# Attention's weighted sum in a decoder layer: one float32 product per head in 32-column tiles, in place of block-diagonal products of split values

## The reference, cut to what matters

```
x = x + attn(layernorm(x))                       # stage A
qh, kh, vh = split(x' @ Wq + bq), split(ctx @ Wk + bk), split(ctx @ Wv + bv)   # 16 heads of 32
scores = einsum('bhqd,bhkd->bhqk', qh, kh) / sqrt(32), causal mask
attn   = softmax(scores)                         # over 77 keys
out    = einsum('bhqk,bhkd->bhqd', attn, vh)     # the weighted sum of the values
x = x + merge(out) @ Wo + bo                     # stage B
x = x + mixture_of_experts(layernorm(x))         # stage C
```

## Time and profile before

| | |
|---|---|
| median of 3 runs | 1202.05 us (1202.03 to 1203.4) |
| span of the profiled execution | 1203.6 us |
| PE busy | 1143.6 us (95%), 5889 products |
| DVE busy | 937.9 us (78%) |
| ACT busy | 737.5 us (61%) |
| POOL busy | 459.2 us (38%) |
| chain that ended last | PE 72%, DVE 9%, DMA 6%, issue 5% |

### The profile page before, as it was taken

How to read it: one execution, slowest core, us unless ns; L and a number is a source line. 1 busy time by engine, 2 the same in 40 slices (tenths; PEclk the granted TensorE clock), 3 DMA queues, 4 the chain that set the end, 5 groups by cost and what they waited for, 6 DMA issues and landing times.

```text
span 1203.6 us, 24087 instructions
## 1 busy us (share of the span) xinstructions
PE 1143.6 (95%) x5889; PEld 962.8 (80%) x5890; DVE 937.9 (78%) x2195; ACT 737.5 (61%) x2114; POOL 459.2 (38%) x412
## 2 busy tenths in 40 slices
PE   6999999999989999999999989999999999999993
PEld 5788888888877888888888767877888888888882
DVE  6788888887775878888868876777777777777774
ACT  4323333233487867768667662766777777778773
POOL 3040000000043333545525254456655555555542
PEclk9999999999999999999979998999999999999998
DMA  8755544345530314153151547886555454444443
GB/s 263 235 155 175 189 168 162 135 165 184 185 122 1 88 53 141 58 136 97 44 140 36 175 144 211 278 210 134 85 83 86 80 87 78 84 81 85 81 66 41
DMA packets 96586, 151.12 MB, mean 126 GB/s; under 512 B 21458, under 2 KB 38038, under 8 KB 95621
## 3 DMA queue, kind: packets, MB, share of 16 engines
q1 hardware_dynamic: 77152, 108.29, 28.7%
q0 software_dynamic: 18528, 39.58, 17.8%
q10 hardware_dynamic: 837, 2.41, 0.6%
HBM read 85.52 MB, written 68.28 MB: 128 GB/s over the span
## 4 chain that ended last, share of the span: by engine, by line
PE 72%; DVE 9%; DMA 6%; issue 5%; POOL 2%; ACT 2%; SPq 1%; DVEq 1%; POOLq 0%; another core or an unknown queue 0%; ACTq 0%
PE banks L1131 26%; PE banks L703 15%; PE banks L768 7%; PE banks L920 6%; DMA out<-rows,scatter_rows 3%; PE banks L873 3%; PE banks L941 2%; PE banks L1143 2%; PE banks L886 2%; PE banks L1159 2%; DVE operands L1614 2%; PE banks L908 2%; ACT rows L1344 1%; ACT operands L1223 1%; PE banks L787 1%
## 5 line engine op out<-in xcount | busy, mean ns | idle before, releaser
L1131 PE MATMUL banks<-operands 128*128 x1608 | 389.8, 397 | 11.4 <-DVE operands L1614 5.2
L1131 PEld LDWEIGHTS banks<-operands 128*128 128x128 f32 x1608 | 298.8, 190 | 74.8 <-issue 8.6
L703 PE MATMUL banks<-operands 128*128 128x512 f32 (+2 forms) x1224 | 293.7, 395 | 8.4 <-DVE operands L1827 4.9
L703 PEld LDWEIGHTS banks<-operands 128*128 128x128 f32 (+1 forms) x1224 | 226.3, 193 | 54.2 <-DVE operands L1827 6.3
L1614 DVE TENSOR_TENSOR operands<-banks,operands 128x512 fp32r<-128x512 f32 (+2 forms) x328 | 220.7, 683 | 44.7 <-ACT operands L1223 37.6
L1223 ACT ACTIVATE operands<-banks 128x512 fp32r<-128x512 f32 (+2 forms) x328 | 191.0, 598 | 92.2 <-PE banks L910 33.2
L1344 ACT ACTIVATE rows<-banks,score_shift 128x77 f32<-128x77 f32 x512 | 159.7, 345 | 10.8 <-DVE score_shift L1836 10.3
L1223 ACT ACTIVATE operands<-rows 128x512 fp32r<-128x512 f32 (+3 forms) x79 | 55.2, 708 | 166.6 <-DVE rows L1685 138.9
L1539 ACT ACTIVATE banks<-banks,param_cols 128x128 f32<-128x128 f32 x268 | 99.2, 430 | 82.2 <-PE banks L1159 79.1
L2681 POOL DMA_INDIRECT out<-rows,scatter_rows x67 | 106.6, 1591 | 101.9 <-DVE rows L2408 65.4
L2600 POOL TENSOR_TENSOR rows<-rows,score_rec 128x1232 f32<-128x1232 f32 x32 | 72.9, 2279 | 170.8 <-DVE score_rec L1844 170.8
(11 more groups left out here) (185 smaller groups left out, 1693.9 us busy)
## 6 DMA issues: line engine op xcount, KB each, us to landing
expert_parts<-operands SPq DMA_DIRECT2D x32, 512.0 KB, 3.0
operands<-expert_parts SPq DMA_DIRECT2D x8, 2048.0 KB, 9.2
rows<-in_x SPq DMA_DIRECT2D x8, 1024.0 KB, 5.4
rows<-in_L_ffn_W SPq DMA_DIRECT2D x32, 256.0 KB, 3.5
x_rows<-rows SPq DMA_DIRECT2D x8, 1024.0 KB, 4.3
rows<-x_rows SPq DMA_DIRECT2D x8, 1024.0 KB, 5.9
xf_rows<-rows SPq DMA_DIRECT2D x32, 256.0 KB, 2.0
out<-rows SPq DMA_DIRECT2D x32, 256.0 KB
```

What stands on the lines that cost most here:

```text
L703: last = nc.tensor.matmul(dst, stationary(a, k), moving(b, k), start=(t == 0 and k == 0), stop=(t == len(terms) - 1 and k == n_k - 1))
L1131: last = nc.tensor.matmul(dst, stationary[:, a, k, :], weights[:, w, bass.ds(e, 1), a2, k, :].rearrange("p e f -> p (e f)"), start=False, ...
```

## The change

The eight products of an `attend` become four, one per head, of operands that are whole float32: weights 77 x 32 (the values of one head, plain rows of `v_keys`), moving operand 77 x 512 (`pT`, one head's probabilities), each into its own 32 partitions of the same bank. The transposes are made head by head: four groups of four, each 128 x 77 in and 77 x 128 out, two groups by a call (`pair`), in place of three. One plain copy out of the bank takes the place of the two splits: by ACT for heads 0 and 2 (`pT_even`), by DVE for heads 1 and 3 (`pT_odd`). `pT` now has two buffers (m % 2), and the semaphore of the banks is cut into three (`features_read`, `pT_by_act`, `pT_by_dve`). The values are stored once as plain rows and loaded once; the zeros, the pieces and the load at the fifth chunk are gone, and so are the splits of the values.

```diff
-        pT = r_at(72.25, 2 * U * CH).rearrange("p (a u t) -> p a u t", a=2, u=U)
-        vblk = r_at(84.25, 2 * KC * U * P).rearrange("p (a m u f) -> p a m u f", a=2, m=KC, u=U)
+        A = nc.alloc_sbuf_tensor_at("whole_operands", [P, 20 * KB_], F32, offset=r_base + 72 * 1024 + 256)
+        pT = A[:, 0:16 * KB_].rearrange("p (i h t) -> p i h t", i=2, h=HPG)
+        v_keys = A[:, 16 * KB_:20 * KB_].rearrange("p (b f) -> p b f", b=B)
...
-            def attend_first(c, m):
-
                 mm_free(c, f"v{m}")
-                pe.wait_ge(vb_in, 16 * (c // CPB + 1))
-                pe.wait_ge(pT_hi, 12 * c + U * m + REST)
-                for u in range(REST):
-                    nc.tensor.matmul(mb(c, f"v{m}"), vblk[:, HI, m, u, :], pT[:, HI, u, :], start=(u == 0), stop=False)
-
-            def attend_rest(c, m):
-
-                for a, a2 in ((LO, HI), (HI, LO)):
-                    if a2 == LO:
-                        pe.wait_ge(b_t_read, t_num(c, f"p{m}{REST}") + 1)
-                    for u in range(REST):
-                        nc.tensor.matmul(mb(c, f"v{m}"), vblk[:, a, m, u, :], pT[:, a2, u, :], start=False, stop=False)
-                for a in (HI, LO):
-                    last = nc.tensor.matmul(mb(c, f"v{m}"), vblk[:, a, m, REST, :], pT[:, HI, REST, :],
-                                            start=False, stop=(a == LO))
+                pe.wait_ge(pT_by_act, pT_read(c, m, 1))
+                pe.wait_ge(pT_by_dve, pT_read(c, m, 1))
+                for hl in range(HPG):
+                    at = (m * HPG + hl) * DH
+                    last = nc.tensor.matmul(mb(c, f"v{m}")[hl * DH:(hl + 1) * DH, :],
+                                            v_keys[0:SK, c // CPB, at:at + DH], pT[0:SK, m % 2, hl, :],
+                                            start=True, stop=True)
                 last.then_inc(mm_done, 1)
...
-                    lo_part(pT[:, LO, u, :], tb(c, f"p{m}{u}"), pT[:, HI, u, :]).then_inc(b_t_read, 1)
+                V.tensor_copy(pT[0:SK, m % 2, hl, :], tb(c, f"p{m}{hl}")[0:SK]).then_inc(pT_by_dve, 1)
...
-                    hi_part(pT[rows, HI, u, :], tb(c, f"p{m}{u}")[rows]).then_inc(pT_hi, 1)
+                nc.scalar.activation(pT[0:SK, m % 2, hl, :], tb(c, f"p{m}{hl}")[0:SK], ACT.Copy).then_inc(pT_by_act, 1)
...
-            n_zero = flat.shape[1] // 8
-            for i in range(8):
-                G.dma_start(flat[:, i * n_zero:(i + 1) * n_zero], zeros_r[:, 0:n_zero].bitcast(F32)).then_inc(zero_out, 16)
```

More of the change, by code:

```diff
@@ L58 @@
 ROUTE_CHOSEN, ROUTE_COUNTED, ROUTE_SHIFTED, ROUTE_WEIGHED, NROUTE = 6, 10, 12, 20, 27
-V_PIECES = [(hl, u, max(NEW_KEY[u] - hl * SK, 0), min(NEW_KEY[u + 1], (hl + 1) * SK) - max(NEW_KEY[u], hl * SK))
-            for hl in range(HPG) for u in range(U) if max(NEW_KEY[u], hl * SK) < min(NEW_KEY[u + 1], (hl + 1) * SK)]
-V_STORES = len(V_PIECES) + sum(u == REST for _, u, _, _ in V_PIECES)
 TERMS = ((HI, HI), (HI, LO), (LO, HI))
@@ L369, in last_in_bank, with rows_read, pT_read, group_before @@
             return in_front(order, c) - len(older) + same[-1] + 1 if same else 0
+        def rows_read(at, i):
+            return 4 * (at + 1) + i + 1
+        def pT_read(c, m, pair):
+            return 8 * c + 2 * m + pair + 1
+        def group_before(c, name):
+            own = groups_of(T_ORDER, c)
+            at = index_in(T_ORDER, c, name)
+            older = [] if isinstance(c, int) and c < 0 else groups_of(T_ORDER, c - 1)
+            row = [(c - 1, g, bank) for g, bank in older] + [(c, g, bank) for g, bank in own[:at]]
+            same = [(turn, g) for turn, g, bank in row if bank == own[at][1]]
+            return same[-1] if same else (c, None)
         def tb(c, name):
@@ L1255, in _ @@
             weight_hi(wg, raw_wg, wg_in, 16)
-            for b in range(B):
-                act.wait_ge(v_ready, b + 1)
-                hi_part(v_r[0:SK, b, HI, :], v_rows[0:SK, b, :]).then_inc(v_hi, 1)
             def h_hi(c, m):
@@ L1346, in exp_scores, with pT_even @@
                                              accum_out=ssum[:, m % 2, at]).then_inc(s_read, 1)
-            def pT_hi_part(c, m, parts):
-                if parts[0] == 0 and m:
-                    act.wait_ge(mm_done, mm_num(c, f"v{m - 1}") + 1)
-                for u in parts:
-                    act.wait_ge(b_t_done, t_num(c, f"p{m}{u}") + 1)
-                    rows = slice(P // 2, P) if u == REST else slice(0, P)
-                    hi_part(pT[rows, HI, u, :], tb(c, f"p{m}{u}")[rows]).then_inc(pT_hi, 1)
+            def pT_even(c, m, pair):
+                if pair == 0 and m >= 2:
+                    act.wait_ge(mm_done, mm_num(c, f"v{m - 2}") + 1)
+                elif pair == 0 and not (isinstance(c, int) and c == 0):
+                    act.wait_ge(mm_done, mm_num(c - 1, f"v{m + 2}") + 1)
+                hl = 2 * pair
+                act.wait_ge(b_t_done, t_num(c, f"p{m}{hl}") + 1)
+                nc.scalar.activation(pT[0:SK, m % 2, hl, :], tb(c, f"p{m}{hl}")[0:SK], ACT.Copy).then_inc(pT_by_act, 1)
             def out_hi(c, m):
@@ L1777, in a_chunk @@
                 for m in (2, 3):
+                    if first and m == 2:
+                        dve.wait_ge(v_out, 16)
                     gated(c, m)
@@ L1806, in _ @@
             w_low(5, wg, raw_wg)
-            for b in range(B):
-                dve.wait_ge(v_hi, b + 1)
-                lo_part(v_r[0:SK, b, LO, :], v_rows[0:SK, b, :], v_r[0:SK, b, HI, :]).then_inc(v_lo, 1)
             dve.wait_ge(consts_done, 1)
@@ L1844, in invert_sums, with pT_odd @@
                 V.reciprocal(srec[:, m % 2, :], ssum[:, m % 2, :]).then_inc(p_rec, 1)
[L1846 to L1853 removed]
+            def pT_odd(c, m, pair):
+                if pair == 0 and m >= 2:
+                    dve.wait_ge(mm_done, mm_num(c, f"v{m - 2}") + 1)
+                elif pair == 0 and not (isinstance(c, int) and c == 0):
+                    dve.wait_ge(mm_done, mm_num(c - 1, f"v{m + 2}") + 1)
+                hl = 2 * pair + 1
+                dve.wait_ge(b_t_done, t_num(c, f"p{m}{hl}") + 1)
+                V.tensor_copy(pT[0:SK, m % 2, hl, :], tb(c, f"p{m}{hl}")[0:SK]).then_inc(pT_by_dve, 1)
             def out_lo(c, m):
```

286 lines of the change are left out of this document (122 added, 164 removed).

## The result

| | median | lowest to highest | runs |
|---|---|---|---|
| before | 1202.57 us | 1202.03 to 1203.4 | 4 |
| after | 1185.43 us | 1185.1 to 1189.34 | 4 |

The ratio is 0.985, with a 95% interval of 0.9813 to 0.9887: the change made the kernel 14 to 22 us faster. The forecast of 1216.5 us had the wrong sign; the time lies inside its wide range, near the first rival (1178 us).

The account below looks back on a forecast made before the run. PE's work was taken to bound stage B, plus 19.3 us of waits. An attend gains 2.20 + 0.15 - 1.95 + 0.30 = +0.70 us; 32 make +22.4, less 8 of waits: +14.4 on 1202.05, 1216.5 us, range 1174 to 1256.

Parts of the forecast that it names:

- first rival: Attends in stage B: all four heads at once, 0.88 us for the products, -19.8 us in all; 1178 us, chance 0.30.
- between the two: Attend: a head's second record holds up the next head, so five steps of 0.44 us, 2.20 us an attend.
- price of a record: Attend: a float32 product of 512 columns is two records of 0.44 us each, 0.88 us a product.
- In and out of narrow products: Attend: going into and out of narrow products adds 0.15 us each time, between 0 and 0.30.
- Transposes: Transposes for an attend: four groups in place of three, +0.30 us, between +0.1 and +0.5.
- Waits: PE's waits in stage B: forecast 8 us back, between 0 and 10; the first rival only 4.
- The clock: Sixth turn of stage B: its fall to the lower clock may go or move; counted 0 in the forecast.
- neither is the bound, so this pays only where PE waits for them: DVE and ACT in stage B: less work pays only through PE's waits, 8 us back of 9.8 for DVE.
- no more than 0.6 us can come of it: Startup: dropping the zero DMAs and value splits saves at most PE's 0.57 us wait for DVE.
- Stage C: Stage C: not touched by the change, expected unchanged within 2 us.
- The second: Attends: products go one behind another, 3.52 us plus 0.15 an attend, +64.6 us less 12; 1255 us, chance 0.24.
- The third: Ends of turns in stage B: the clock falls, 7.6 us a turn, up to 45 us more; 1262 us, chance 0.12.

Follow-up runs that it names:

- experiment 1: Kernel after, each of an attend's four products given 128 columns of weights and writing all 128 partitions, over the one before; 1256.1 us, ratio 1.0453.
- experiment 4: Kernel after, each attend's four products issued twice, head by head (0, 0, 1, 1, 2, 2, 3, 3); 1215.77 us, ratio 1.0124 to the kernel before.
- experiment 2: Kernel after, the four 32-column products of an attend all writing partitions 0 to 31; 1263.25 us, ratio 1.0499 to the kernel before.
- experiment 6: Kernel before, DVE making low parts of the probabilities for only 16 of 512 columns, PE's work untouched; 1191.12 us, ratio 0.9907.
- experiment 7: Kernel after, DVE copying the bank of head 1 a second time into a buffer nobody reads; 1192.49 us, ratio 0.9925 to the kernel before.
- experiment 12: Kernel before, unchanged, run and profiled once more; 1199.38 us in one run.
- experiment 10: Kernel after, the eight DMAs of zeros put back at the start on POOL; 1189.08 us, ratio 0.9884 to the kernel before.
- experiment 8: Kernel after, second transposes of group 1 spread around the scores of group 3; 1182.67 us, ratio 0.9843 to the kernel before.
- experiment 9: Kernel after, group 1's second transposes spread, and in the first turn two tiles of group 2's scores ahead of x1's transposes; 1188.75 us, ratio 0.9877.

## Why the prediction failed, point by point

**The step that failed** is the one "between the two": "the second record of a head must go through the columns that the first still uses", and so five steps of 0.44 us, 2.20 an attend. The price of a record was right (0.43 measured, experiment 1). The order was wrong: each set of 32 columns takes its records without holding up the others (windows of 544.60 to 545.30, experiment 4), so it is two steps, 0.86 us. The reason that I gave, that every row in order of time shows starts in program order, holds for full-width products only, which all use the same columns; it could not tell the two cases apart. This step alone is worth 32 x (2.20 - 0.86) = 43 us of the sum, and it turned the sign.

**The mis-sized terms**, against the first rival's sum (0.88 + 0.15 - 1.95 + 0.30 = -0.62 an attend, -19.8 in all):

- In and out of narrow products: 0.15 foreseen; about 0.26 measured, namely 0.12 to 0.14 inside the attend, 0.09 ahead of it and 0.05 behind it (experiments 1 and 2). With 0.10 ahead of it an attend is 1.10; what stands behind it is in the next term. The Trainium skill ("TensorEngine Tiling (Array Packing)", Key Properties) says that a change of the tiling mode drains TensorE; the trace agrees in that going in and out costs these 0.26 us, and doesn't show the drain itself.
- Transposes: 0.30 foreseen, 0.52 measured. A group of four takes 0.40 to 0.43 us in place of 0.36, and there are 16 in a turn in place of 12: 6.55 us in place of 4.47. The weight loads take 148 ns, no less than the 141 before, so fewer columns there gave nothing: the upper end of the range was right.
- So an attend with its transposes is 1.10 - 1.95 + 0.52 = -0.33, and 32 of them -10.6 us, half of the rival's -19.8.
- Waits: 4 us back foreseen by the rival, 3.9 measured (19.3 to 15.4). That the numbers agree is luck: it is a sum of 4.9 us that went, 7.1 that came at a place that I hadn't looked at, and smaller ones that went. The new wait was to be seen in the order of the instructions ahead of the run: two groups behind one pair of x1's.
- The clock: counted as 0, it was -7.6 in this pair of profiles. In sum -10.6 - 3.9 - 7.6 = -22.1 for stage B, where -20.1 was measured. The medians hold an unknown share of the clock: runs of the kernel before on one chip lie 9 to 18 us apart, and the shorter ones have the higher mean granted clock (0.991 at 1193.58 us, 0.977 at 1211.16).

**The other engines**: "neither is the bound, so this pays only where PE waits for them" put relief on DVE at 8 us of waits. Its worth is about right, 7 to 10 us (experiments 6 and 7), but in experiment 7 the price is not paid in waits for DVE. What was paid in those runs is short falls of the clock and turns longer by some tenths; why DVE's load should cost that way stays open.

**Startup and stage A**: "no more than 0.6 us can come of it" was too narrow, since it looked at one wait only. In both profiles of the kernel before PE waits three times for DVE by 93 us: 0.6 (1.5 in experiment 12), 0.8 and 0.2; after, it never does. From the start of the 108 products to the third set of transposes behind them (L741, L745 after) it is 63.8 and 64.75 us before and 61.8 after. The likely reason is that DVE's splits of the values were felt up to 60 us later, in its queue; no run put them back alone. With the 1.6 us of an earlier start, which is chance (experiment 10), this makes 3.6 of the 3.9 us.

**Stage C**: +3.7 us, foreseen unchanged within 2. Measured from its second transposes to the end it takes 483.4 and 483.1 us in the profiles of before, 485.3 in experiment 6, 487.7 and 485.6 in those of after, and 482.9 to 490.5 in those of its variants. The variants do the same there, so most of this belongs to the execution and not to the change; a part of 1 or 2 us that comes of the change isn't excluded.

**The rivals**: the first, with a chance of 0.30, was what happened, and its 1178 us were too low by the terms above. The second is what the products would cost in the same columns (1256 and 1263 measured, 1255 foreseen). The third is real as a mechanism at the place it named, the end of a turn, but at 1.6 to 3.3 us a fall and not 7.6, in some turns and not in all. The kernel after was free of it in stage B in both its profiles, and several of its variants were not.

**Left open**: what decides whether the clock falls in a turn. It did in turns with 0 to 0.25 us of idle PE (experiments 8 and 9), but not in others of the same runs, nor in those of experiment 6, in which PE was idle for nothing in three turns; and it did in turns with 1 us of idle time (experiments 4, 7 and 10).

## What to carry to other kernels

If each of several small products fills only a part of TensorE's columns, give each its own set of columns and issue them in a row: here they went beside each other for one product's time, in both orders of the queue that were tried, and also when a product needs two passes. Price such a change with its neighbours: here the products gave 27 us, of which the extra transposes took 17 back, and the rest of the gain came with fewer waits, less work for DVE and the clock. A wait of PE that is removed may be lost again to the clock (experiments 8 and 9); look at the granted clock by turn before you count it.

## What the runs showed of the hardware

- A plain float32 product over 512 columns is two records of 0.43 us each, with 128 columns of weights as with 32 (3.43 and 3.55 us for four products).
- Four such products with 32 columns each, in different columns, take 1.00 us together, two take 0.98, and eight 1.86 or 1.88, by turns or head by head: a product starts ahead of an earlier one that must wait for its own columns (experiment 4).
- Going into and out of products of 32 columns costs about 0.26 us: 0.09 ahead, 0.12 within, 0.05 behind (experiments 1 and 2).
- Weight loads of 32 columns of float32 values take 106 ns, of 128 columns 193 (experiment 1). Those of the transposes take 148 ns with 77 columns and 140 to 145 with 128; all eight loads of an attend lie within 0.16 us (0.03 and 0.13 in the windows).
- The granted clock fell at the end of some turns, at a loss of 1.6 to 7.6 us a turn, in kernels with and without narrow products. In the kernel before it came in the sixth turn in one execution and near the end of stage B in the next.
